# Differential attention: its outputs turned by head group and four tiles, and the output stage run as one sequence of 16 tiles

## The chip, the cores and the metric

The kernel runs on one core of a Trainium2 chip. The metric is the time of one execution on the device in microseconds (us), lower is better. The core has a matmul engine (TensorE, PE in the rows, with its weight loads as PEld), VectorE (DVE), ScalarE (ACT), GpSimd (POOL) and SyncE (SP), which issues the DMAs.

## The reference

The input is 16 sequences of 1024 tokens with 256 features. Four blocks follow one another, each on a layernorm of its input and added to it: a local attention, a feed-forward block, a differential attention, the same feed-forward block. The change lies in the third, which is this (cut):

```python
def _L0_attn_b_ref(x, Wq, Wk, Wv, Wo, lambda_q1, ..., subln_g):
    H, hd = 16, 8
    q = rope((x @ Wq).reshape(b, s, 2 * H, hd))      # 32 heads of 8
    k = rope((x @ Wk).reshape(b, s, 2 * H, hd))
    v = (x @ Wv).reshape(b, s, H, 2 * hd)            # 16 heads of 16
    probs = softmax(q k^T / sqrt(hd))                # per head, 1024 x 1024
    w = probs[:, :, 0] - lam * probs[:, :, 1]        # heads in pairs
    attn = w @ v
    rms = rsqrt(mean(attn * attn, -1) + EPS)
    attn = attn * rms * subln_g * (1.0 - LAMBDA_INIT)
    return attn.reshape(b, s, 256) @ Wo
```

## The kernel before, in words

A loop runs eight times, each time over a pair of sequences (`PB` = 2). A sequence has 8 tiles of 128 tokens (`T`), a pair 16 (`TT`). In each round stand layernorm, local attention, layernorm, `ffn`, layernorm, `diff_project` and `diff_attention`, `diff_output`, layernorm, `ffn`. The order of work on each engine is written out by hand; engines wait for each other by semaphores.

**The rotation.** `diff_attention` works on 16 groups (`PB * NG`) of four heads (`G`), eight per sequence. A clock of steps `e` runs over all of them, 32 steps (`STEPS`) to a group, 512 in all (`LAST`). In a step TensorE makes, alternating, two matmuls of exponent scores (`exp_scores`, L1203) for this step and two of max scores (`max_scores`, L1181) for the step `AHEAD` = 39 later, and then half of the value matmuls of a unit (`values`, eight per step in the rows, L1221). ScalarE makes two exponentials per step (L1339), VectorE one maximum over 1024 scores (L1257). In 39 steps at the end there are no max scores any more. The unnormalised outputs with their row sums stand in one PSUM bank per half group; ScalarE copies them to `oT` (`keep_output`, L1359), features in partitions, two steps into the next group. The next value matmuls wait for that copy. Once in a group, GpSimd cuts the maxima in three parts (`cut`), TensorE turns them (L1189) and SyncE stores them.

**Turning the outputs.** 32 units are needed in a pair to bring outputs back to tokens in partitions: each is four transposes of 128 x 128 into one PSUM bank (`turned_heads`, L1004). Before, a unit is one tile of 128 tokens for four head groups, so it needs all eight of a sequence's groups in two halves, numbered `j` = 0 to 15. Behind the transposes comes a chain: divide by the row sums, subtract lambda times the second head of each pair, mean square, inverse root, multiply, write to `attended`.

- The 16 units of the first sequence are *early*: they stand in the rotation at steps 6 and 15 of groups 4 to 11 (`EARLY`). The turn takes one of the three banks of the exponent scores, ScalarE copies it out (`keep_raw`, L1348), and GpSimd does the whole chain (`early`, L1305 to L1316).
- 8 units of the second sequence stand in the tail, from step `ALONE` on, one in four steps (`output_step`). Their chain is shared: VectorE `combine` (L1016, L1018, L1025), GpSimd `square` (L1032), VectorE `mean_square` (L1036, L1038), GpSimd `inverse_root` (L1042), VectorE `normalise` (L1050).
- The last 8 stand in `diff_output`, with the same chain.

**The output stage.** `diff_output` is a block of its own: for each tile TensorE transposes the two 128-column halves of `attended` (`features`, L1385), ScalarE copies them to `aT` (`keep`, L1450), TensorE multiplies by `wo` in two accumulating matmuls (`project`, L1393, four instructions in the rows), VectorE adds to `x` (`residual`, L1415) and takes the layernorm statistics (`statistics`, L1420). Its loop runs over tiles `t` of both sequences at once, the second two tiles behind. Each sequence has one PSUM bank for its projection, so `project(b, t)` waits for `residual(b, t - 1)`:

```python
for t in range(T + 5):
    if t < T:
        combine(v, T + t)
    if 1 <= t <= T:
        mean_square(v, T + t - 1)
    if 2 <= t < T + 2:
        normalise(v, T + t - 2)
    if 2 <= t < T + 2:
        residual(0, t - 2)
    if 3 <= t < T + 3:
        statistics(0, t - 3)
    if 4 <= t < T + 4:
        residual(1, t - 4)
```

## Time and profile before

| | |
|---|---|
| Median of three runs | 9148.5 us (9129.78 to 9150.74) |
| Profiled execution | 9143.53 us, its span 9141.9 us |
| TensorE, matmuls | 7776.9 us busy, 85% |
| VectorE | 7227.1 us, 79% |
| ScalarE | 6201.5 us, 68% |
| GpSimd | 2700.3 us, 30% |
| TensorE's mean granted clock | 0.924 |

Times in a timeline are microseconds from the start of the span. A row of several instructions (x4) gives the start of the first and the time to the end of the last; matmuls are pipelined, so the next row can start before it ends. In brackets stands how long the engine was idle before the row, and what released it. A granted clock of 1.0 is 2.4 GHz, 0.5 is 1.2 GHz.

### The profile page before, as it was taken

The numbers are of one execution on the slowest core, as the hardware profiler recorded it, in microseconds if no ns is written. First come the engines' busy times: TensorE is split into PE (matmuls) and PEld (weight loads), VectorE is DVE, ScalarE is ACT, GpSimd is POOL, SyncE is SP. The second block draws the span as 40 slices with busy tenths as digits, with TensorE's granted clock in tenths as the row PEclk, the third lists the DMA queues.
The fourth block names the chain that finished last, engine by engine and source line by source line (L and its number), as shares of the span: only waits on it lengthen the run. The fifth ranks groups of instructions, "written<-read, shape, count | busy, mean of one in ns | idle before, by whom it ended". The sixth has DMA issues, their size and how long they took to land. (4 is left out here: it accounts for less than half of the span.)

```text
span 9141.9 us, 163324 instructions
## 1 busy us (share of the span) xinstructions
PE 7776.9 (85%) x65408; PEld 2851.3 (31%) x65408; DVE 7227.1 (79%) x9490; ACT 6201.5 (68%) x11410; POOL 2700.3 (30%) x3046
## 2 busy tenths in 40 slices
PE   6799877998779987799877998779977799777997
PEld 3222342223422234222342223422234222342223
DVE  5899558995589955899558995589955899558995
ACT  4499544995449954499544995449955499554995
POOL 3233241332413324133241332413324133241322
PEclk9899987999879998799988999889999799897998
DMA  0100001000010000100001000010000100001000
GB/s 28 42 23 23 10 10 42 23 23 10 10 42 23 23 12 9 42 23 23 14 7 45 23 20 16 5 46 23 19 17 4 46 23 19 19 1 46 23 19 19
DMA packets 216827, 204.98 MB, mean 22 GB/s; under 512 B 105783, under 2 KB 141111, under 8 KB 216055
## 3 DMA queue, kind: packets, MB, share of 16 engines
q1 hardware_dynamic: 216060, 194.46, 7.4%
q8 instruction: 519, 8.50, 0.4%
q14 instruction: 248, 2.02, 0.1%
HBM read 123.83 MB, written 67.37 MB: 21 GB/s over the span
## 5 line engine op out<-in xcount | busy, mean ns | idle before, releaser
L1257 DVE TENSOR_REDUCE mfull<-ps 128x1 f32<-128x1024 f32 x4096 | 4692.9, 1217 | 225.1 <-PE ps L1181 220.7
L1339 ACT ACTIVATE work<-ps 128x512 f32<-128x512 f32 x8192 | 4385.6, 597 | 346.9 <-PE ps L1203 225.0
L1221 PE MATMUL ps<-work,vbuf 128*32 128x256 f32 x32768 | 2623.2, 392 | 116.6 <-ACT hh L1359 116.6
L1181 PE MATMUL ps<-kop,qop 48*128 48x512 bf16 x8192 | 2507.2, 394 | 59.1 <-DVE mfull L1257 51.7
L1203 PE MATMUL ps<-qop,kop 51*128 51x512 bf16 x8192 | 2489.2, 384 | 0.0
L1221 PEld LDWEIGHTS ps<-work,vbuf 128*32 128x32 f32 x32768 | 654.3, 108 | 1800.9 <-issue 896.0
L1203 PEld LDWEIGHTS ps<-qop,kop 51*128 51x128 bf16 x8192 | 482.2, 93 | 1649.6 <-ACT work L1339 1585.9
L1287 POOL CAST mpart<-mfull 128x32 bf16<-128x32 f32 x128 | 27.0, 211 | 2541.6 <-DVE mfull L1257 2363.6
L1305 POOL TENSOR_TENSOR work<-work,none 128x16 f32<-128x16 f32 x128 | 371.7, 2904 | 1014.4 <-ACT work L1348 1014.4
L263 PE MATMUL ps<-ident,hh 128*128 128x128 f32 x1024 | 200.0, 373 | 510.4 <-DVE hh L233 510.4
L416 POOL TENSOR_TENSOR hh<-work,hmask 128x1024 f32<-128x1024 f32 x256 | 522.1, 2065 | 129.7 <-PE ps L344 129.6
L1181 PEld LDWEIGHTS ps<-kop,qop 48*128 48x128 bf16 x8192 | 473.2, 94 | 218.3 <-DVE mfull L1257 190.5
L816 POOL TENSOR_TENSOR work<-work,vbuf 128x1024 f32<-128x1024 f32 x64 | 194.6, 3041 | 884.0 <-DVE work L731 884.0
L272 ACT COPY hh<-ps 128x512 f32<-128x512 f32 x128 | 75.1, 587 | 492.1 <-PE ps L263 492.1
L518 ACT COPY vbuf<-qop 32x512 f32<-32x512 f32 x512 | 315.5, 616 | 116.7 <-DVE qop L461 107.2
L609 PE MATMUL ps<-work,w 128*128 128x512 f32 x768 | 371.3, 623 | 12.9 <-ACT work L674 6.6
L1016 DVE RECIPROCAL work<-ps 128x16 f32<-128x16 f32 x128 | 32.8, 257 | 411.6 <-PE ps L1004 411.6
L263 PEld LDWEIGHTS ps<-ident,hh 128*128 128x128 f32 x1024 | 174.1, 196 | 534.3 <-DVE hh L233 520.7
L882 PE MATMUL ps<-wv,hh 128*128 128x256 f32 x512 | 215.0, 561 | 141.1 <-DVE work L911 141.1
L361 PE MATMUL ps<-vbuf,work 128*32 128x128 f32 x4096 | 162.0, 306 | 182.2 <-ACT hh L523 175.3
L729 DVE TENSOR_TENSOR hh<-work,vbuf 128x1024 f32<-128x1024 f32 x128 | 156.2, 1220 | 172.4 <-ACT vbuf L667 172.4
L1393 PE MATMUL ps<-wo,work 128*128 128x256 f32 x512 | 191.0, 515 | 113.4 <-DVE x L1415 113.4
(163 smaller groups left out, 9125.6 us busy)
## 6 DMA issues: line engine op xcount, KB each, us to landing
qop<-scratch SPq DMA_DIRECT2D x512, 64.0 KB
scratch<-work SPq DMA_DIRECT2D x32, 768.0 KB, 3.6
scratch<-hh SPq DMA_DIRECT2D x32, 768.0 KB, 4.6
kop<-scratch SPq DMA_DIRECT2D x256, 96.0 KB
vbuf<-in_x SPq DMA_DIRECT2D x9, 2048.0 KB, 8.3
qop<-scratch SPq DMA_DIRECT2D x512, 32.0 KB
kop<-scratch SPq DMA_DIRECT2D x256, 64.0 KB
out<-x SPq DMA_DIRECT2D x64, 256.0 KB, 2.1
```

The costliest lines, as they stand in the source:

```text
L263: mm = pe.transpose(ps[:, 4 * (t // T) + c * NB + t % T // 4, at:at + P], h[:, t, c * P:(c + 1) * P], ident[:, :])
L416: pool.tensor_tensor(kx[i % len(kx)], qkT[:, b, 2 + c, tb * P:(tb + 1) * P][:, None, :].to_broadcast([P, LC, P]), hmask[:, :, None].to_bro ...
L518: act.copy(PT[t % 2][r, :, r], pr[t % 2][r]).then_inc(s_pa, 1)
L609: mm = pe.matmul(ps[:, 2 * n, :], w2[:, c, :], a1[n][:, c, :], start=c == 0, stop=c == C - 1)
L816: pool.tensor_tensor(U[n], U[n], cr[0][n][:, None, :].to_broadcast([P, C, HALF]), ALU.mult).then_inc(s_q, 1)
L882: mm = pe.matmul(ps[:, 4 + t // 2, (t % 2) * D:(t % 2 + 1) * D], hT[:, b, c, t * P:(t + 1) * P], wv[:, c, :], start=c == 0, stop=c == C - 1)
L1181: pe.matmul(ps[:, b + n, :], qop[r:r + KQ, s, i, t * P:(t + 1) * P], kop[r:r + KQ, s, i, half(n)], start=True, stop=True).then_inc(s_ms, 1)
L1203: pe.matmul(ps[:, bank, :], kop[r:r + KM, s, i, t * P:(t + 1) * P], qop[r:r + KM, s, i, half(n)], start=True, stop=True).then_inc(s_sc, 1)
L1221: mm = pe.matmul(ps[VW * i:VW * (i + 1), OB, cols], vp[:, b, t, (G * gl + i) // 2, :], prob[:, u % PS, i, cols], start=t == 0 and part == ...
L1257: v.tensor_reduce(mfull[:, g % 2, r // ROWS, i * T + t:i * T + t + 1], ps[:, b:b + NB, :].rearrange("p b n -> p (b n)"), AX.X, ALU.max).th ...
L1305: link(pool.tensor_tensor(erz, y[:, :, LD], none[:, :], ALU.pow))
L1339: act.activation(prob[:, u % PS, hl, :], ps[:, EB[slot % len(EB)], :], ACT.Exp, scale=scale).then_inc(s_ex, 1)
```

## The change

A unit is now one head group for four tiles (`side` 0 or 1 of its sequence), so it can be turned as soon as its own group is finished. Early are all units of groups 0 to 13 (`FIRST` = 14): 28 of them, each pair at steps 6 and 15 of the group that follows. The units of group 14 stand at steps 6 and 10 of the last group (`LATE`), those of group 15 in `diff_output`. There the loop runs over 16 tiles in one sequence, features two tiles ahead of projections, with two banks for the projections and four for the features; all but two units' chains are gone from it.

```diff
+        FIRST = PB * NG - 2
         def output_bank(j):
...
-        def turned_heads(pe, bank, j):
-            g0, t = NG // 2 * (j // T), j % T
-            for g in range(g0, g0 + NG // 2):
-                mm = pe.transpose(ps[:, bank, (g - g0) * P:(g - g0 + 1) * P],
-                                  oT[:, g, t * P:(t + 1) * P], ident[:, :])
+        def turned_heads(pe, bank, g, side):
+            for t in range(T // 2):
+                at = (side * T // 2 + t) * P
+                mm = pe.transpose(ps[:, bank, t * P:(t + 1) * P], oT[:, g % NG, at:at + P], ident[:, :])
             return mm
...
         def turn_output(pe, j):
-            if j % T >= 2:
+            if j >= 2:
                 pe.wait_ge(s_nm, j - 1)
-            turned_heads(pe, output_bank(j), j).then_inc(s_tp, 1)
+            turned_heads(pe, output_bank(j), FIRST + j // 2, j % 2).then_inc(s_tp, 1)
...
-        def heads_of(b, t, c):
-            return attended[:, b, t, c * P:(c + 1) * P].rearrange("p (v d) -> p v d", d=LD)
+        def normalised(eng, g, side, by, root):
+            b, cols = g // NG, slice(g % NG * 2 * LD, (g % NG + 1) * 2 * LD)
+            dst = attended[:, b, side * T // 2:(side + 1) * T // 2, cols].rearrange("p t (v d) -> p t v d", d=LD)
+            factor = root.rearrange("p (t v) -> p t v", v=2)[:, :, :, None].to_broadcast([P, T // 2, 2, LD])
+            return eng.tensor_tensor(dst, by.rearrange("p (t v) d -> p t v d", v=2), factor, ALU.mult)
         def normalise(v, j):
-            t, c = j % T, j // T
             v.wait_ge(s_pw, j + 1)
-            v.tensor_tensor(heads_of(1, t, c), diff[j % 3],
-                            rr[:, j, :][:, :, None].to_broadcast([P, HV, LD]), ALU.mult).then_inc(s_an, 1)
+            normalised(v, FIRST + j // 2, j % 2, diff[j % 3], rr[:, j, :]).then_inc(s_an, 1)
...
             HQ = HALF // 2
-            ALONE = LAST - AHEAD + 4
-            EARLY = [STEPS * g + o for g in range(NG // 2, NG // 2 + NG) for o in (6, 15)]
+            EARLY = [STEPS * (g + 1) + o for g in range(FIRST) for o in (6, 15)]
+            LATE = [STEPS * (FIRST + 1) + o for o in (6, 10)]
             scale = DD ** -0.5
...
-            def output_step(e):
-                j = e - ALONE
-                return j // 4 if j % 4 == 0 and 0 <= j < 4 * T else None
             def value_tile(e):
...
                     def early_turn(j):
-                        pe.wait_ge(s_oe, NB * NG // 2 * (j // T + 1))
-                        turned_heads(pe, bank_for(turn_slot(j)), j).then_inc(s_sc, 1)
+                        pe.wait_ge(s_oe, NB * (j // 2 + 1))
+                        turned_heads(pe, bank_for(turn_slot(j)), j // 2, j % 2).then_inc(s_sc, 1)
...
                                 values(tile_due(e, part), part)
-                        if output_step(e) is not None:
-                            if output_step(e) == 0:
+                        if e in LATE:
+                            if e == LATE[0]:
                                 pe.wait_ge(s_mts, GROUPS)
-                            turn_output(pe, output_step(e))
+                                pe.wait_ge(s_oe, NB * (FIRST + 1))
+                            turn_output(pe, LATE.index(e))
...
                         reduce(m)
-                    for j in range(T + 2):
-                        if j < T:
-                            combine(v, j)
-                        if 1 <= j <= T:
-                            mean_square(v, j - 1)
-                        if j >= 2:
-                            normalise(v, j - 2)
+                    for step in (combine, mean_square, normalise):
+                        for j in range(2):
+                            step(v, j)
...
                         link(pool.tensor_tensor(err, esv, nhalf[:, 0:HV], ALU.pow))
-                        link(pool.tensor_tensor(heads_of(0, j % T, j // T), ediff,
-                                                err[:, :, None].to_broadcast([P, HV, LD]), ALU.mult))
+                        link(normalised(pool, j // 2, j % 2, ediff, err))
...
                             early(EARLY.index(e))
-                    for j in range(T + 1):
-                        if j < T:
-                            square(pool, j)
-                        if j >= 1:
-                            inverse_root(pool, j - 1)
+                    for step in (square, inverse_root):
+                        for j in range(2):
+                            step(pool, j)
...
-            s_wt, s_we, s_wm, s_wx = ([sem(f"do_{n}{b}") for b in range(PB)] for n in ("wt", "we", "wm", "wx"))
+            s_wt, s_we, s_wm, s_wx = (sem(f"do_{n}") for n in ("wt", "we", "wm", "wx"))
             with nc.Block() as block:
...
                 def _(pe):
-                    def features(b, t, c):
-                        if b:
-                            pe.wait_ge(s_an, c * T + t + 1)
-                        if t >= 2 and c == 0:
-                            pe.wait_ge(s_we[b], t - 1)
-                        pe.transpose(ps[:, 4 + 2 * b + t % 2, c * P:(c + 1) * P], attended[:, b, t, c * P:(c + 1) * P],
-                                     ident[:, :]).then_inc(s_wt[b], 1)
+                    def features(t):
+                        if t == T:
+                            pe.wait_ge(s_an, 4)
+                        if t >= 4:
+                            pe.wait_ge(s_we, t - 3)
+                        for c in range(C):
+                            mm = pe.transpose(ps[:, 4 + t % 4, c * P:(c + 1) * P],
+                                              attended[:, t // T, t % T, c * P:(c + 1) * P], ident[:, :])
+                        mm.then_inc(s_wt, 1)
-                    def project(b, t):
-                        pe.wait_ge(s_we[b], t + 1)
-                        if t >= 1:
-                            pe.wait_ge(s_wx[b], t)
+                    def project(t):
+                        pe.wait_ge(s_we, t + 1)
+                        if t >= 2:
+                            pe.wait_ge(s_wx, t - 1)
                         for c in range(C):
-                            mm = pe.matmul(ps[:, 2 + b, 0:D], aT[:, b, c, t * P:(t + 1) * P],
+                            mm = pe.matmul(ps[:, 2 + t % 2, 0:D], aT[:, t // T, c, t % T * P:(t % T + 1) * P],
                                            wo[:, c, :], start=c == 0, stop=c == C - 1)
-                        mm.then_inc(s_wm[b], 1)
+                        mm.then_inc(s_wm, 1)
-                    for t in range(T + 3):
-                        if t < T:
-                            turn_output(pe, T + t)
-                            for c in range(C):
-                                features(0, t, c)
-                        if 1 <= t <= T:
-                            project(0, t - 1)
-                        if 2 <= t < T + 2:
-                            for c in range(C):
-                                features(1, t - 2, c)
-                        if t >= 3:
-                            project(1, t - 3)
+                    for j in (2, 3):
+                        turn_output(pe, j)
+                    for t in range(TT + 2):
+                        if t < TT:
+                            features(t)
+                        if t >= 2:
+                            project(t - 2)
...
                 def _(v):
-                    def residual(b, t):
-                        tt = T * b + t
-                        v.wait_ge(s_wm[b], t + 1)
-                        v.tensor_tensor(x[:, tt, :], x[:, tt, :], ps[:, 2 + b, 0:D], ALU.add).then_inc(s_wx[b], 1)
-                    def statistics(b, t):
-                        tt = T * b + t
-                        v.wait_ge(s_wx[b], t + 1)
-                        v.bn_stats(st[:, tt, :], x[:, tt, :])
-                    for t in range(T + 5):
-                        if t < T:
-                            combine(v, T + t)
-                        if 1 <= t <= T:
-                            mean_square(v, T + t - 1)
-                        if 2 <= t < T + 2:
-                            normalise(v, T + t - 2)
-                        if 2 <= t < T + 2:
-                            residual(0, t - 2)
-                        if 3 <= t < T + 3:
-                            statistics(0, t - 3)
-                        if 4 <= t < T + 4:
-                            residual(1, t - 4)
-                        if t >= 5:
-                            statistics(1, t - 5)
+                    def residual(t):
+                        v.wait_ge(s_wm, t + 1)
+                        v.tensor_tensor(x[:, t, :], x[:, t, :], ps[:, 2 + t % 2, 0:D], ALU.add).then_inc(s_wx, 1)
+                    def statistics(t):
+                        v.wait_ge(s_wx, t + 1)
+                        v.bn_stats(st[:, t, :], x[:, t, :])
+                    for step in (combine, mean_square):
+                        for j in (2, 3):
+                            step(v, j)
+                    for t in range(TT + 1):
+                        if t < TT:
+                            residual(t)
+                        if t >= 1:
+                            statistics(t - 1)
+                        if t in (1, 2):
+                            normalise(v, t + 1)
...
                 def _(pool):
-                    for t in range(T + 1):
-                        if t < T:
-                            square(pool, T + t)
-                        if t >= 1:
-                            inverse_root(pool, T + t - 1)
+                    for step in (square, inverse_root):
+                        for j in (2, 3):
+                            step(pool, j)
...
                 def _(act):
-                    def keep(b, t):
-                        act.wait_ge(s_wt[b], C * (t + 1))
-                        act.copy(aT[:, b, :, t * P:(t + 1) * P],
-                                 ps[:, 4 + 2 * b + t % 2, 0:D].rearrange("p (c n) -> p c n", c=C)).then_inc(s_we[b], 1)
-                    for t in range(T + 2):
-                        if t < T:
-                            keep(0, t)
-                        if t >= 2:
-                            keep(1, t - 2)
+                    for t in range(TT):
+                        act.wait_ge(s_wt, t + 1)
+                        act.copy(aT[:, t // T, :, t % T * P:(t % T + 1) * P],
+                                 ps[:, 4 + t % 4, 0:D].rearrange("p (c n) -> p c n", c=C)).then_inc(s_we, 1)
```

TensorE in the rotation, at steps 5 and 6 of group 1 (L1004 and L1006 are the turn; L1203, L1181, L1221 before are L1200, L1178, L1218 now). Before:

```order
L1203 MATMUL ps<-qop,kop 128x512
L1181 MATMUL ps<-kop,qop 128x512
L1221 MATMUL ps<-work,vbuf 32x256 x4
L1203 MATMUL ps<-qop,kop 128x512
L1181 MATMUL ps<-kop,qop 128x512
```

and now:

```order
L1200 MATMUL ps<-qop,kop 128x512
L1178 MATMUL ps<-kop,qop 128x512
L1218 MATMUL ps<-work,vbuf 32x256 x4
L1006 MATMUL ps<-ident,hh 128x128 x4
L1200 MATMUL ps<-qop,kop 128x512
L1178 MATMUL ps<-kop,qop 128x512
```

A turn has moved in between the value matmuls of a step and the scores of the next, here and at step 15, in groups 1 to 3 and 12 to 14 too.

TensorE at the start of `diff_output` (L1004, now L1006, turns outputs; L1385, now L1376, are features; L1393, now L1385, projections). Before:

```order
L1004 MATMUL ps<-ident,hh 128x128 x4
L1385 MATMUL ps<-ident,work 128x128 x2
L1004 MATMUL ps<-ident,hh 128x128 x4
L1385 MATMUL ps<-ident,work 128x128 x2
L1393 MATMUL ps<-wo,work 128x256 x2
L1004 MATMUL ps<-ident,hh 128x128 x4
L1385 MATMUL ps<-ident,work 128x128 x2
L1393 MATMUL ps<-wo,work 128x256 x2
```

and now:

```order
L1006 MATMUL ps<-ident,hh 128x128 x8
L1376 MATMUL ps<-ident,work 128x128 x6
L1385 MATMUL ps<-wo,work 128x256 x2
L1376 MATMUL ps<-ident,work 128x128 x2
L1385 MATMUL ps<-wo,work 128x256 x2
```

Six of eight turns have left the block; the other two stand ahead of everything.

VectorE in `diff_output`, from the chain of one new unit to the next (L1016, L1018, L1025 are `combine`, L1036 and L1038 `mean_square`, L1050 `normalise`, L1415 `residual`, L1420 `statistics`). Before:

```order
L1016 RECIPROCAL work<-ps 128x16
L1018 TENSOR_TENSOR work<-ps,work 128x256
L1025 SCALAR_TENSOR_TENSOR work<-work,nlam 128x128
L1036 TENSOR_REDUCE work<-work 128x8
L1038 TENSOR_SCALAR work<-work 128x8
L1050 TENSOR_TENSOR work<-work 128x128
L1415 TENSOR_TENSOR x<-x,ps 128x256
L1420 BN_STATS st<-x 128x6
L1415 TENSOR_TENSOR x<-x,ps 128x256
L1420 BN_STATS st<-x 128x6
```

and now, from the second `mean_square` on (L1037, L1039; L1049 is `normalise`, L1401 `residual`, L1405 `statistics`):

```order
L1037 TENSOR_REDUCE work<-work 128x8
L1039 TENSOR_SCALAR work<-work 128x8
L1401 TENSOR_TENSOR x<-x,ps 128x256 x2
L1405 BN_STATS st<-x 128x6
L1049 TENSOR_TENSOR work<-work 128x4x32
L1401 TENSOR_TENSOR x<-x,ps 128x256
L1405 BN_STATS st<-x 128x6
L1049 TENSOR_TENSOR work<-work 128x4x32
L1401 TENSOR_TENSOR x<-x,ps 128x256
L1405 BN_STATS st<-x 128x6
```

After that only residuals and statistics alternate, where six more rounds of the chain stood between them.

## Rows read from the trace of the kernel before

**Rows 1.** View by stretch: rotation, output stage of the second pair.

```profile
1530.00:2142.70 612.70, 590.81 (x6176) 155.40 (x6173) 555.67 (x522) 566.83 (x1087) 165.53 (x283) 0.99 0.07 19
2142.70:2190.40 47.70, 32.08 (x128) 24.97 (x128) 24.59 (x80) 5.97 (x16) 16.27 (x16) 0.79 0.00 1
```

**Rows 2.** Timeline of TensorE in the rotation (start us, length us, engine, line, operation).

```profile
1685.32 0.64 PE L1221 MATMUL ps<-work,vbuf 128*32 128x256 f32 x8 [0.48 <-ACT hh L1359]
...
1687.54 0.64 PE L1221 MATMUL ps<-work,vbuf 128*32 128x256 f32 x8
1688.11 0.66 PE L1004 MATMUL ps<-ident,hh 128*128 128x128 f32 x4
...
1689.23 0.64 PE L1221 MATMUL ps<-work,vbuf 128*32 128x256 f32 x8
```

**Rows 3.** Timeline of the rotation's tail: TensorE, and ScalarE's last output copy.

```profile
2132.68 0.64 PE L1221 MATMUL ps<-work,vbuf 128*32 128x256 f32 x8
...
2134.37 0.64 PE L1221 MATMUL ps<-work,vbuf 128*32 128x256 f32 x8
...
2142.05 0.59 ACT L1359 COPY hh<-ps 128x512 f32<-128x512 f32 x1 [1.19 <-PE ps L1221]
```

**Rows 4.** Timeline of TensorE in the output stage.

```profile
2142.95 0.63 PE L1004 MATMUL ps<-ident,hh 128*128 128x128 f32 x4 [0.96 <-PEq L1133]
2143.41 0.38 PE L1385 MATMUL ps<-ident,work 128*128 128x128 f32 x2
...
2144.28 1.10 PE L1393 MATMUL ps<-wo,work 128*128 128x256 f32 x4
...
2173.34 1.56 PE L1393 MATMUL ps<-wo,work 128*128 128x256 f32 x4 [2.10 <-DVE x L1415]
2174.69 0.63 PE L1385 MATMUL ps<-ident,work 128*128 128x128 f32 x2
2175.12 1.92 PE L1393 MATMUL ps<-wo,work 128*128 128x256 f32 x4
2176.83 0.82 PE L1004 MATMUL ps<-ident,hh 128*128 128x128 f32 x4
...
2184.53 0.38 PE L1385 MATMUL ps<-ident,work 128*128 128x128 f32 x2
2184.75 1.03 PE L1393 MATMUL ps<-wo,work 128*128 128x256 f32 x4
2185.62 0.38 PE L1385 MATMUL ps<-ident,work 128*128 128x128 f32 x2
...
2188.09 1.10 PE L1393 MATMUL ps<-wo,work 128*128 128x256 f32 x4 [0.61 <-DVE x L1415]
```

**Rows 5.** Timeline of VectorE in the output stage.

```profile
2148.38 0.41 DVE L1415 TENSOR_TENSOR x<-x,ps 128x256 f32<-128x256 f32 x1
...
2171.07 0.26 DVE L1016 RECIPROCAL work<-ps 128x16 f32<-128x16 f32 x1 [3.49 <-PE ps L1004]
...
2172.79 0.41 DVE L1415 TENSOR_TENSOR x<-x,ps 128x256 f32<-128x256 f32 x1
...
2187.53 0.42 DVE L1415 TENSOR_TENSOR x<-x,ps 128x256 f32<-128x256 f32 x1 [0.62 <-PE ps L1393]
...
2189.23 0.42 DVE L1415 TENSOR_TENSOR x<-x,ps 128x256 f32<-128x256 f32 x1 [0.95 <-PE ps L1393]
2189.57 0.74 DVE L1420 BATCH_NORM_STATS2 st<-x 128x6 f32<-128x256 f32 x2
```

**Rows 6.** Timeline of GpSimd in the rotation: a unit's chain, the next chain.

```profile
1689.33 2.92 POOL L1305 TENSOR_TENSOR work<-work,none 128x16 f32<-128x16 f32 x1 [14.44 <-ACT work L1348]
...
1698.11 0.40 POOL L1316 TENSOR_TENSOR work<-work 128x128 f32<-128x128 f32 x1
1699.87 2.91 POOL L1305 TENSOR_TENSOR work<-work,none 128x16 f32<-128x16 f32 x1 [1.36 <-ACT work L1348]
```

**Rows 7.** Groups by line: busy us, mean ns of one, idle us before and releaser.

```profile
L1348 ACT COPY work<-ps 128x272 f32<-128x272 f32 x128 | 49.4, 386 | 39.4 <-PE ps L1004 39.4
```

## The prediction

> **What bounds the kernel now.** I read the page's head first (no engine is busy for more than 85% of the span, so the change must be priced stage by stage), then busy time by stretch, then the timeline of the second of the eight pairs, engine by engine. The view by stretch gives the length, the busy time of TensorE, its weight loads, VectorE, ScalarE and GpSimd, and TensorE's granted clock. The two stretches that it touches are the rotation (1530.0 to 2142.7 us) and the output stage (2142.7 to 2190.4 us). In the rotation TensorE is busy 590.8 of 612.7 us, and its clock is granted at 0.99; in the output stage it is busy 32.1 of 47.7 us at 0.79, so it sits idle for a third of the time and runs at 1.2 GHz for part of it [rows 1].
>
> In the rotation one step lasts 1.11 us (two of them from the value matmuls at 1685.32 to those at 1687.54). The step that holds a turn of attention outputs lasts 1.69 us (1687.54 to 1689.23): its four transposes push everything behind them back by 0.58 us [rows 2]. So the matmul queue sets the pace there, and nothing hides a turn. In the tail, where the max scores have ended, a step with a turn lasts 1.69 us as well (2132.68 to 2134.37) [rows 3].
>
> The output stage is the slow one. One round of its loop makes one turn and takes a tile of each sequence through features and projection, and in each TensorE waits for `residual` on VectorE before the second sequence's projection: 2.10 us at 2173.34, for one [rows 4]. VectorE is late because `residual` of the first sequence stands in its queue behind the whole chain of a new unit (`combine`, `mean_square`, `normalise`): L1016 starts at 2171.07 and the residual L1415 at 2172.79, 1.72 us later [rows 5]. The matmuls of a round themselves are short at 2.4 GHz: features to projection 0.22 us (2184.53 to 2184.75), projection to next features 0.87 us (2184.75 to 2185.62), so 1.09 us a tile. At 1.2 GHz they take 0.43 and 1.71 us, 2.14 us a tile (2174.69, 2175.12, 2176.83) [rows 4].
>
> **The change, part by part.**
>
> *Turns in the rotation.* Both versions turn 32 units of four transposes in a pair. Before, 16 are early, 8 are in the tail and 8 in the output stage; now 28 are early, 2 in the tail and 2 in the output stage. The rotation holds 30 instead of 24, so it grows by 6 x 0.58 = 3.5 us. Bounds: 6 x 0.46 = 2.8 us by the turn in the output stage (2142.95 to 2143.41 [rows 4]) and, if each of the 12 added early turns also cost ScalarE's copy of 0.39 us, 3.5 + 4.7 = 8.2 us. I take 3.5, because the early turn of [rows 2] already carries that copy [rows 7] and costs the same as one in the tail, which has none. The order within the turn (four tiles of one head group, not four groups of one tile) leaves count and shape alone.
>
> *Waits of the added turns.* Each now follows the output copy of its own group, where before four groups lay between. The last value matmul that waited for that copy goes at 1685.32, and the first turn of the group stands at 1688.11, 2.8 us later [rows 2]. The wait is over by then: nothing. GpSimd's chain for a unit runs 1689.33 to 1698.51, 9.2 us, and the next one begins 1.36 us after it [rows 6]. The added chains keep those places, steps 6 and 15 of 32, with `cut` of the maxima at step 24 behind them, so what holds in groups 4 to 11 holds in the new ones. `normalised` writes four pieces of 32 columns instead of one of 128; were its 0.40 us to double, the 1.36 us would still cover it. In the six groups that get chains anew, GpSimd was idle.
>
> *Tail.* Two units at step 6 and 10 of the last group, so VectorE and GpSimd finish their chains well before ScalarE's last copy ends at 2142.64 (2142.05 + 0.59 [rows 3]). Nothing.
>
> *Output stage.* Before, it lasts from 2142.64 to the end of the last statistics, 2189.57 + 0.74 = 2190.31: 47.7 us [rows 5]. Now:
> - TensorE starts at 2142.95 as before. Two turns at 0.46 (2142.95 to 2143.41 [rows 4]): 0.92. The first projection starts 0.87 after the first features (2143.41 to 2144.28, with ScalarE's copy between): projection 0 at 2144.74, projection 1 at 2144.74 + 1.09 = 2145.83.
> - Projection 2 needs residual 0. Before, the first residual starts at 2148.38, behind three units' `combine`; now two stand ahead of it, which takes the 1.72 us of one unit out of the queue: 2146.7. TensorE goes on 0.56 us after a residual starts (2187.53 to 2188.09 [rows 4, 5]): 2147.3, where its own queue would have come to it at 2146.9, a wait of 0.4 us.
> - From there nothing holds TensorE. Per tile VectorE needs at most 0.41 us for the residual and 0.37 for the statistics (0.74 for two) [rows 5], and ScalarE's one copy fits into the 0.87 us from features to projection above, against 1.09. A projection's bank comes back in time: the residual starts about 0.26 us after the last matmul has issued (2188.09 + 0.87 = 2188.96; 2189.23) and TensorE goes 0.56 later, 0.82 in all, while the next tile covers 0.22 + 0.87 + 0.22 = 1.31 us.
> - `normalise` of the last two units ends at the latest two units after that first residual, 2146.7 + 2 x 1.72 = 2150.1. The first features of the second sequence go after projection 5, near 2151.4. This wait costs nothing.
> - Projections 3 to 13: 11 x 1.09 = 12.0; the last two without features 2 x 0.87 = 1.7: projection 15 at 2161.0. From there to the end of statistics 2.22 us (2188.09 to 2190.31): 2163.3.
> That is 20.6 us; 0.4 for handovers that I cannot see makes 21.0. Bounds: 20.2 without the early wait and the allowance; 40.5 at 1.2 GHz throughout (below).
>
> *Clock.* The sum takes 2.4 GHz. In the output stage of before, with waits of 2.10 us in TensorE's queue [rows 4], its mean is 0.79, and matmuls of the same kind issue in 0.43 us after such a wait and in 0.22 late in the stage; in the rotation, where TensorE is busy for 96% of the time, it is 0.99 [rows 1]. The new stage has one gap of about 1 us at the start, as before, one of 0.4, and then none. A rule of the Trainium skill speaks against this: "TensorE: Matmul & The Clock Gate", section "A second HAM failure mode: psum-queue depth-cycling", says that cycling through PSUM banks in each iteration can leave gaps small and many enough for the clock to swing between its two levels. The new stage does cycle two and four banks. By that rule the sum would come out as rival 1; the rotation cycles seven banks and keeps its clock, which is why I hold to the row.
>
> *What stays.* Layernorm, ffn, local attention, the projections and all DMAs are untouched; SP's queue holds the same.
>
> **Sum.** Per pair 47.7 - 21.0 - 3.5 = 23.2 us; x 8 = 186 us. I take off 2 us because not every pair need be as long as this one: 184 us. The profiled execution took 9143.5 us, so 8960 us. The median of the three runs lies 5 us higher; I say **8962 us**, 2.0% less.
>
> **Rivals.**
> 1. *The clock falls in the output stage.* At the share of low clock of before (mean 0.79) the stage's 19 us of matmul work become 19 / 0.79 = 24: +5 us a pair, +40: about 9002 us. At 1.2 GHz throughout, a tile costs 2.14 instead of 1.09, over some 18 tile lengths +19 us a pair, +152: 9114 us, still 0.4% faster. For: the clock of before does swing there. Against: it fell after waits that are gone. Chance 0.15, nearly all of it on the mild form.
> 2. *The turns cost more in the rotation.* If every early turn waited for its output copy by the 0.48 us of [rows 2], 28 x 0.48 = 13 us a pair, +108: 9070 us. Against: 2.8 us of distance. Chance 0.03.
> 3. *Slower: the hand-back stays in series.* If a projection in the new stage still waits 2.10 us for its residual, as in every period of before, now with every tile, a tile costs 1.09 + 2.10 = 3.2 us; 16 x 3.2 + 4 = 55 us, 7.5 more than now, and with the 3.5 of the rotation 11 us a pair: +88, about 9232 us. It decides from a tile length of (47.7 - 3.5 - 4) / 16 = 2.5 us on. For: projections use two banks and wait for the residual two tiles back. Against: that wait came from the chains queued ahead of the residual, of which two are left, both at the start. Chance 0.02.
> 4. *The change does nothing there*, because something that I don't see bounds the stage, 9140 us: 0.02.
>
> **How the numbers follow.** Forecast 0.78, rivals 0.15, 0.03, 0.02, 0.02. The low end is the sum with the lower bounds, 0.8 us a pair for the stage and 0.8 for the turns (-13), and the spread of the runs shown (14 us below the profiled one): 8938. The high end takes in the mild clock case and some more of low clock, 9035. A measurement here can tell about 0.3% from no change, 27 us. Faster by more than that: forecast, rivals 1 and 2, 0.96; within it 0.02; slower 0.02.
>
> **What would show it.** Right: in the profile of the changed kernel the stage from ScalarE's last output copy to the last statistics takes about 21 us, with projections (L1385) 1.09 us apart, a granted clock near 1.0 in it and no wait of 2.10 us; groups 1 to 3 and 12 to 14 of the rotation are 1.16 us longer each, and the tail has two steps of 1.69 us. Wrong: a tile length of 2.1 us (clock), a wait for `residual` at each tile (rival 3), or a wait before the turns in the rotation.

## The result, and the profile after

| | before | after |
|---|---|---|
| median | 9149.62 us (4 runs, 9129.78 to 9152.19) | 8992.63 us (4 runs, 8968.44 to 9000.3) |
| profiled execution | 9143.53 us | 8998.98 us, its span 8997.5 us |

The ratio is 0.983, with a 95% interval of 0.9812 to 0.9849: 157 us less, where 186 us were forecast. The time, 8992.6 us, lies inside the range of 8938 to 9035 us and 31 us above the 8962 us forecast. The changed kernel is 1.7% faster, and a ratio of 1 lies far outside the interval. What has to be found out is where these 31 us went (29 by the differences). The two profiled executions are 144.5 us apart and not 157, so they show some 13 us more missing than the medians do.

The busy time by stretch of the changed kernel, for the same pair as [rows 1], columns as there (length, busy time and count of TensorE, weight loads, VectorE, ScalarE and GpSimd, TensorE's granted clock, DMA share, GB/s). First the output stage, then the rotation with what leads up to its first exponential:

```profile
2140.60:2161.00 20.40, 18.91 (x104) 15.80 (x104) 15.30 (x44) 5.77 (x16) 4.04 (x4) 1.00 0.00 0
1524.00:2140.60 616.60, 594.37 (x6202) 157.51 (x6200) 547.04 (x487) 570.97 (x1099) 252.57 (x415) 0.99 0.07 19
```

The stage went from 47.70 to 20.40 us, and its clock from 0.79 to 1.00, which is 2.4 GHz throughout. TensorE is busy there for 93% of the time, against 67% before. GpSimd's sixteen steps have become four.

The timeline of all engines from the last output copy (L1350) into the stage answers to [rows 4, 5]. Columns: start, length, engine, line and operation, tiles, count, and the idle time before with its releaser:

```profile
2139.94 0.59 ACT L1350 COPY hh<-ps 128x512 f32<-128x512 f32 x1 [1.19 <-PE ps L1218]
2140.84 1.06 PE L1006 MATMUL ps<-ident,hh 128*128 128x128 f32 x8 [0.96 <-PEq L1130]
...
2142.58 1.13 PE L1385 MATMUL ps<-wo,work 128*128 128x256 f32 x4
...
2143.77 1.03 PE L1385 MATMUL ps<-wo,work 128*128 128x256 f32 x4
...
2144.53 0.74 DVE L1401 TENSOR_TENSOR x<-x,ps 128x256 f32<-128x256 f32 x2
...
2145.09 1.10 PE L1385 MATMUL ps<-wo,work 128*128 128x256 f32 x4
...
2146.25 1.03 PE L1385 MATMUL ps<-wo,work 128*128 128x256 f32 x4
...
2150.57 0.42 DVE L1401 TENSOR_TENSOR x<-x,ps 128x256 f32<-128x256 f32 x1 [0.33 <-PE ps L1385]
2150.59 1.03 PE L1385 MATMUL ps<-wo,work 128*128 128x256 f32 x4
...
2151.67 1.03 PE L1385 MATMUL ps<-wo,work 128*128 128x256 f32 x4
```

Two things are to be seen. The projections (L1385) stand 1.08 to 1.09 us apart once the stage runs (2150.59, 2151.67), and now VectorE waits for TensorE (0.33 us), not TensorE for VectorE: the 2.10 us of [rows 4] are gone. The projection of tile 2 at 2145.09 comes 1.32 us behind that of tile 1 at 2143.77, so the one wait at the start that the sum allowed for is about 0.2 us instead of 0.4.

In the rotation the added turns look like the old ones. The timeline of TensorE around the first turn of group 1, where none stood before, and of GpSimd behind it, answers to [rows 2, 6]:

```profile
1568.10 0.64 PE L1218 MATMUL ps<-work,vbuf 128*32 128x256 f32 x8 [0.48 <-ACT hh L1350]
...
1570.32 0.64 PE L1218 MATMUL ps<-work,vbuf 128*32 128x256 f32 x8
1570.88 0.66 PE L1006 MATMUL ps<-ident,hh 128*128 128x128 f32 x4
1571.47 0.39 PE L1200 MATMUL ps<-qop,kop 51*128 51x512 bf16 x1
...
1572.01 0.64 PE L1218 MATMUL ps<-work,vbuf 128*32 128x256 f32 x8
```

```profile
1572.11 2.91 POOL L1299 TENSOR_TENSOR work<-work,none 128x16 f32<-128x16 f32 x1 [14.44 <-ACT work L1339]
...
1580.90 0.40 POOL L1049 TENSOR_TENSOR work<-work 128x128 f32<-128x128 f32 x1
1582.66 2.91 POOL L1299 TENSOR_TENSOR work<-work,none 128x16 f32<-128x16 f32 x1 [1.35 <-ACT work L1339]
```

The step with a turn lasts 1.69 us (1570.32 to 1572.01). The last value matmul that waited for the group's output copy (the 0.48 us) goes 2.8 us before the turn, and the turn has no wait of its own. GpSimd's chain still takes 9.2 us, its last write 0.40 us although it now goes in four pieces, and 1.36 us are left to the next. By the starts of ScalarE's exponentials, groups 1 to 3, 12 and 13 of this pair are 1.1 to 1.3 us longer than before, group 14 is 0.58 longer (one of the tail's turns stood in it before) and the last group is 2.9 us shorter (39.9 to 36.9 us from its first exponential to its last), which is five turns of 0.58 less.

**The stages of the whole loop.** From the first and last rows of each stage (statistics L244, first exponential, last output copy, last statistics of the output stage) follow these lengths, means over the eight pairs in us; the last column, up to L244 of the next round, over seven:

| | layernorm, local | layernorm, ffn | layernorm, project | rotation | output stage | layernorm, ffn, back to the top |
|---|---|---|---|---|---|---|
| before | 133.2 | 112.0 | 117.0 | 612.5 | 47.4 | 116.5 |
| after | 135.4 | 112.4 | 117.5 | 615.9 | 20.4 | 119.5 |
| difference | +2.2 | +0.4 | +0.5 | +3.3 | -27.0 | +2.9 |

The two stages that were priced give 27.0 - 3.3 = 23.7 us a pair, against 23.2 forecast. The rest was taken as unchanged and is not: 8 x (2.2 + 0.4 + 0.5) + 7 x 2.9 = 45 us. 8 x 23.7 - 45 = 145 us is the difference of the two spans (9141.9 and 8997.5 us, 144.4).

**The last column.** The idle time of VectorE before the round's first instruction (L242), all executions of it, by what ended it (us, times). Before:

```profile
  PEq L1472: 34.7, 7
```

After:

```profile
  issue: 55.4, 7
```

"issue" means that nothing in the profile held the engine. One execution of it in the timeline of VectorE, before and after:

```profile
2305.59 1.17 DVE L242 BATCH_NORM_AGGREGATE mv<-st 128x2 f32<-128x6 f32 x16 [4.97 <-PEq L1472]
```

```profile
2279.18 1.17 DVE L242 BATCH_NORM_AGGREGATE mv<-st 128x2 f32<-128x6 f32 x16 [7.89 <-issue]
```

That is 3 us a round, 20.7 us over the seven. The records of control instructions say where: from the branch that closes the loop to the first instruction of the next round (a hint to prefetch, which stands at the top of each round on every engine) VectorE takes 0.52 to 0.59 us before and 2.82 to 3.50 us after, while the other engines take 0.25 to 0.47 us in both. VectorE's loop body has shrunk from 1257 to 1173 instructions, because the chains of twelve units are no longer VectorE's but GpSimd's.

**The first three columns.** They differ with TensorE's granted clock, and within one execution too. By stretch, changed kernel: one pair's projection at a low and one at a higher clock, then two local attentions:

```profile
4774.27:4891.28 117.01, 85.45 (x242) 37.81 (x243) 93.03 (x90) 25.20 (x30) 35.31 (x18) 0.73 0.23 75
5891.22:6003.21 111.99, 80.23 (x242) 35.01 (x243) 92.93 (x90) 25.21 (x30) 35.31 (x18) 0.82 0.23 78
...
4526.23:4661.59 135.36, 104.09 (x1184) 69.58 (x1184) 82.39 (x189) 66.51 (x108) 78.57 (x37) 0.85 0.00 1
5646.73:5779.76 133.03, 100.88 (x1184) 66.45 (x1184) 81.86 (x189) 66.50 (x108) 78.61 (x37) 0.90 0.01 1
```

The kernel before, two local attentions:

```profile
3446.80:3579.47 132.67, 100.44 (x1184) 66.17 (x1184) 81.88 (x189) 66.57 (x108) 78.59 (x37) 0.90 0.01 1
5723.31:5858.89 135.58, 103.82 (x1184) 69.49 (x1184) 82.48 (x190) 66.57 (x108) 78.56 (x37) 0.85 0.01 1
```

The same instructions take 132.7 or 135.6 us in both kernels, with TensorE's busy time 3 us apart and everybody else's nearly equal. Before, seven of eight pairs were of the short kind; after, one of eight.

### The profile page after: what moved, and what is told of

The parts are those of the page before. It is cut to its first block and busy times, and to the rows that moved or that the text cites. A ratio compares the mean times of both kernels' runs of the same rounds, so it can differ in the third digit from the quotient of the medians.

```text
span 8997.5 us, 163868 instructions
## 1 busy us (share of the span) xinstructions
PE 7715.0 (86%) x65408; PEld 2815.5 (31%) x65408; DVE 7091.0 (79%) x8914; ACT 6231.5 (69%) x11506; POOL 3298.5 (37%) x4006
## 5 line engine op out<-in xcount | busy, mean ns | idle before, releaser
L1218 PE MATMUL ps<-work,vbuf 128*32 128x256 f32 x32768 | 2623.2, 392 | 118.6 <-ACT hh L1350 118.6
L1178 PE MATMUL ps<-kop,qop 48*128 48x512 bf16 x8192 | 2506.0, 395 | 58.6 <-DVE mfull L1255 51.7
L1200 PE MATMUL ps<-qop,kop 51*128 51x512 bf16 x8192 | 2487.8, 384 | 0.0
L1299 POOL TENSOR_TENSOR work<-work,none 128x16 f32<-128x16 f32 x224 | 650.4, 2904 | 1775.4 <-ACT work L1339 1775.4
L1218 PEld LDWEIGHTS ps<-work,vbuf 128*32 128x32 f32 x32768 | 654.3, 108 | 1807.0 <-issue 916.7
L1200 PEld LDWEIGHTS ps<-qop,kop 51*128 51x128 bf16 x8192 | 478.4, 93 | 1634.4 <-ACT work L1330 1577.2
L1178 PEld LDWEIGHTS ps<-kop,qop 48*128 48x128 bf16 x8192 | 470.9, 94 | 217.8 <-DVE mfull L1255 190.8
L1309 POOL TENSOR_TENSOR work<-work,nhalf 128x8 f32<-128x8 f32 x224 | 373.8, 1669 | 18.7
L255 POOL TENSOR_TENSOR rstd<-rstd,nhalf 128x16 f32<-128x16 f32 x32 | 93.0, 2908 | 513.7 <-DVE rstd L244 513.7
```

The costliest lines, as they stand in the source:

```text
L1178: pe.matmul(ps[:, b + n, :], qop[r:r + KQ, s, i, t * P:(t + 1) * P], kop[r:r + KQ, s, i, half(n)], start=True, stop=True).then_inc(s_ms, 1)
L1200: pe.matmul(ps[:, bank, :], kop[r:r + KM, s, i, t * P:(t + 1) * P], qop[r:r + KM, s, i, half(n)], start=True, stop=True).then_inc(s_sc, 1)
L1218: mm = pe.matmul(ps[VW * i:VW * (i + 1), OB, cols], vp[:, b, t, (G * gl + i) // 2, :], prob[:, u % PS, i, cols], start=t == 0 and part == ...
L1299: link(pool.tensor_tensor(erz, y[:, :, LD], none[:, :], ALU.pow))
L1309: link(pool.tensor_tensor(err, esv, nhalf[:, 0:HV], ALU.pow))
```

## The experiments

The kernel before ran beside the others each time, so its median moves a little: 9156.73 us (7 runs) for e1 to e4, 9145.4 (9 runs) for e5 to e7, 9163.36 (one run) for e8 and e9. The theory that was tested first: VectorE's 3 us are a fetch of instructions at the back edge (the branch from the end of the loop to its top), caused by where the shorter body ends, not by the work in it.

**e1: the head of the loop put at slot 0.** A slot is a position in the engine's instruction stream, counted modulo 256 (a fetch block, below). Nothing else changes.

```diff
-        with nc.Fori(0, PAIRS, hint_back_edge=True) as q:
+        with nc.Fori(0, PAIRS, hint_back_edge=True, head_slot={mybir.EngineType.DVE: 0}) as q:
```

> The changed kernel, with VectorE's loop body loaded from another place (slot 0 of a fetch block); no instruction is added or taken. Theory A: the 3.0 us that VectorE needs in the changed kernel from the loop's closing branch to the first instruction of the next round (0.5 us in the kernel before) is a fetch of instructions that comes too late because of where the closing branch stands in a fetch block. Then it falls to about 0.5 us, the stretch from the last statistics of the output stage to the next round's layernorm from 119.4 to 116.5 us, and the time by about 20 us, to 8970 us. Rival B: it comes from the change's own instructions in the loop, wherever they stand; then it stays at 3.0 us and the time at 8990 us.

Measured: 8969.26 us (4 runs, 8964.76 to 8973.06), ratio to the kernel before 0.9794 (0.9778 to 0.981). From branch to next instruction 0.52 to 0.59 us in every round, and the last column is back at 116.4 us. VectorE's idle time before L242:

```profile
  PEq L1444: 34.5, 7
  issue: 3.6, 1
```

The single "issue" of 3.6 us is the entry into the loop, paid once. Medians: 23 us less than the changed kernel. The 3 us a round hang on the position of the code alone.

**e2: the length of the body brought back.** 84 instructions (168 waits on a value long reached, two to an instruction) ahead of VectorE's late chains, where it waits anyway.

```diff
                     for m in range(LAST):
                         reduce(m)
+                    for k in range(168):
+                        v.wait_ge(s_mr, LAST - k)
                     for step in (combine, mean_square, normalise):
```

> The changed kernel with 84 instructions more on VectorE (waits that have long been met), placed in the tail of the rotation where VectorE is idle, so that its loop has as many instructions as before (1257). Theory A: the branch stands where it stood before, and VectorE goes on after 0.5 us instead of 3.0; stretch of 116.5 us. Rival B: 3.0 us stay. Rotation and output stage as in the changed kernel (616 and 20.4 us).

Measured: 8955.91 us (one run), body 1257 instructions as before, 0.5 to 0.6 us at every back edge, last column 116.4 us. More instructions, less time.

**e3: the kernel before, with 172 instructions added.** The body is then 1429 long, which is 1173 + 256, so its end falls on the same slot of a block as that of the changed kernel.

```diff
                         if j >= 2:
                             normalise(v, j - 2)
+                        if j < T:
+                            for k in range(44 if j < 4 else 42):
+                                v.wait_ge(s_mr, LAST - k)
```

> The kernel before with 172 such waits more on VectorE, in its idle gaps in the tail, so that its closing branch stands at the same place of a fetch block as in the changed kernel (1429 instructions = 1173 + 256). Theory A: the stall of 3.0 us appears in the kernel before too, and its stretch from the last statistics to the next layernorm grows from 116.5 to 119.4 us. Rival B: 0.5 us as in the kernel before. Output stage 47.7 us in both.

Measured: 9162.42 us (one run). VectorE's idle time before L242:

```profile
  issue: 54.8, 7
```

The stall of the changed kernel (55.4 us in seven rounds), in the kernel that never had it; the last column is 119.4 us. The output stage took 46.3 us (47.4 before) and the whole time lies within what the kernel before showed beside it (9135.26 to 9164.75 us), so the stall is read from its own gap and not from the time. With e1 and e2 it is shown from both sides. A second reading: local attention took 134.6 us on average here against 133.2, though its code is the old one. So a good part of the +2.2 us in the first column comes without the change's work.

**e4: one bank for the projections instead of two.** Each projection then waits for the residual of the tile before.

```diff
-                        if t >= 2:
-                            pe.wait_ge(s_wx, t - 1)
+                        if t >= 1:
+                            pe.wait_ge(s_wx, t)
...
-                            mm = pe.matmul(ps[:, 2 + t % 2, 0:D], ...
+                            mm = pe.matmul(ps[:, 2, 0:D], ...
```

> The changed kernel with one PSUM bank instead of two for the projections of the output stage, so that each projection waits for the residual of the tile just before. Theory: the tile length is set by TensorE's own 1.08 us only while the hand-back (0.26 + 0.56 us after the matmuls) is hidden behind the next tile; with one bank a tile becomes 0.87 + 0.26 + 0.56 = 1.7 us, the stage 20.4 + 13 x 0.62 = 28 to 30 us, if the clock stays high; if the gap of 0.6 us a tile lets the clock fall, tiles of 2.5 us and a stage of up to 42 us. Rival: the second bank does not matter, since features stand between two projections: 20.4 us.

Measured: 9066.55 us (one run). The stage takes 30.7 us, a little over the 28 to 30 expected, a tile 1.70 to 1.71. The timeline of TensorE, and the stage by stretch:

```profile
2153.17 1.10 PE L1385 MATMUL ps<-wo,work 128*128 128x256 f32 x4 [1.16 <-DVE x L1401]
2154.11 0.38 PE L1376 MATMUL ps<-ident,work 128*128 128x128 f32 x2
2154.87 1.10 PE L1385 MATMUL ps<-wo,work 128*128 128x256 f32 x4 [0.39 <-DVE x L1401]
```

```profile
2148.60:2179.30 30.70, 22.21 (x104) 16.02 (x104) 15.30 (x44) 5.78 (x17) 4.04 (x4) 1.00 0.00 0
```

Each tile is 1.70 - 1.09 = 0.61 us longer (the idle time in brackets is 0.39 of it), worth 10.2 us a pair with the longer wait at the start: the second bank is what takes the hand-back out of series. And the clock stays at 1.00 although TensorE is busy for only 72% of the stage, hardly more than the 67% at 0.79 before. Busy share alone does not tell the two apart; what does, these rows leave open.

**e5: one transpose of four in each early turn.** Leaves out three of four tiles in every early unit; ScalarE's copy keeps its size.

```diff
-        def turned_heads(pe, bank, g, side):
-            for t in range(T // 2):
+        def turned_heads(pe, bank, g, side, tiles=T // 2):
+            for t in range(tiles):
...
-                        turned_heads(pe, bank_for(turn_slot(j)), j // 2, j % 2).then_inc(s_sc, 1)
+                        turned_heads(pe, bank_for(turn_slot(j)), j // 2, j % 2, 1).then_inc(s_sc, 1)
...
-                        act.copy(raw[j % 2], src[:, :, 0:LD + 1]).then_inc(s_ex, 1)
+                        act.copy(raw[j % 2].rearrange("p (t k) w -> p t k w", k=4),
+                                 src[:, None, :, :].to_broadcast([P, 4, 4, LD + 1])).then_inc(s_ex, 1)
```

> The changed kernel with one transpose instead of four in each of the 28 early turns; ScalarE copies the one turned tile four times into the same buffer (same size of copy), GpSimd's chain is unchanged. What is left out: three of four tiles of these outputs. Theory: the price of a turn in the rotation is TensorE's transposes, so that three of four gone take 28 x 0.44 = 12.3 us from the rotation (616.0 to about 604 us a pair). Rival: ScalarE's copy of 0.39 us, hidden behind them, takes their place; then a turn still costs 0.3 us and the rotation falls by 7 to 8 us only, to 608. A second rival, that GpSimd's chains or their contention set the price: 616 stay.

Measured: 8910.61 us (one run). The rotation takes 607.1 us, 8.8 less, 0.31 us for each of 28 turns. By the starts of ScalarE's exponentials a group of 32 steps takes 37.23 us without turns (kernel before), 38.39 with two, and 37.78 here: 0.58 and 0.28 us a turn. The time falls between the two theories, nearer to the rival's 608. TensorE's timeline around the same turn as above:

```profile
1555.07 0.64 PE L1218 MATMUL ps<-work,vbuf 128*32 128x256 f32 x8
1555.64 0.33 PE L1006 MATMUL ps<-ident,hh 128*128 128x128 f32 x1
1555.90 0.39 PE L1200 MATMUL ps<-qop,kop 51*128 51x512 bf16 x1
...
1556.43 0.64 PE L1218 MATMUL ps<-work,vbuf 128*32 128x256 f32 x8
```

From the first transpose to the next scores TensorE takes 0.26 us with one transpose (1555.64 to 1555.90) and 0.59 with four (1570.88 to 1571.47), and neither row of scores shows a wait. So a turn does not cost four equal parts: three transposes less save 0.33 us, 28 x 0.33 = 9.2 us against 8.8 measured, and the 0.26 that is left stands in TensorE's own queue. The theory's number missed because it took 0.44 of the 0.58 off; the rival's number came close, but no wait for ScalarE's copy is needed to explain it. ScalarE has no idle time before its copy of this turn (0.29 us in the changed kernel), so a limit set by ScalarE may lie close below; that was not tried.

**e6: eight units in the output stage again, with the new order of tiles.** Eight of the 32 units stand in the output stage, as before, one per tile (the other 24 are early, none is in the tail), with their chains on VectorE and GpSimd; the sequence of 16 tiles and the banks stay.

```diff
-        FIRST = PB * NG - 2
+        FIRST = PB * NG - 4
...
-                    for j in (2, 3):
-                        turn_output(pe, j)
                     for t in range(TT + 2):
+                        if t < T:
+                            turn_output(pe, t)
                         if t < TT:
                             features(t)
...
-                    for t in range(TT + 1):
-                        if t < TT:
-                            residual(t)
-                        if t >= 1:
-                            statistics(t - 1)
-                        if t in (1, 2):
-                            normalise(v, t + 1)
+                    for t in range(TT + 3):
+                        if t < T:
+                            combine(v, t)
+                        if 1 <= t <= T:
+                            mean_square(v, t - 1)
+                        if 2 <= t <= T:
+                            normalise(v, t - 2)
+                        if t == T:
+                            normalise(v, T - 1)
+                        if 2 <= t < TT + 2:
+                            residual(t - 2)
+                        if t >= 3:
+                            statistics(t - 3)
```

> The changed kernel with 8 units in the output stage, as in the kernel before (24 early, none in the tail), each turned ahead of the features of one of the first 8 tiles, its chain queued ahead of the residuals; the order of 16 tiles, two banks for projections and four for features stay. It splits the gain of the output stage between the chains that left and the new order. Theory that the chains ahead of the residuals set the stage: the first 8 tiles cost 2.4 us each by VectorE's queue (1.7 for the chain, 0.7 for residual and statistics), the stage 8 x 2.4 + 8 x 1.1 + 3 = 31 us and more if the clock falls in the waits (37). Rival, that the old order with one bank a sequence was the loss: 20.4 + 6 x 0.5 of turns = 24 us. Rotation 612.5 us, as before.

Measured: 9063.14 us (one run), the stage 34.7 us on average, between the 31 and the 37 us expected, the rotation 612.4. TensorE's timeline, and the stage by stretch:

```profile
2144.01 1.10 PE L1377 MATMUL ps<-wo,work 128*128 128x256 f32 x4 [0.64 <-DVE x L1393]
...
2158.60 0.69 PE L1368 MATMUL ps<-ident,work 128*128 128x128 f32 x2 [6.67 <-DVE work L1049]
2159.08 1.91 PE L1377 MATMUL ps<-wo,work 128*128 128x256 f32 x4
2160.78 0.64 PE L1368 MATMUL ps<-ident,work 128*128 128x128 f32 x2
2161.21 1.37 PE L1377 MATMUL ps<-wo,work 128*128 128x256 f32 x4
```

```profile
2137.10:2171.30 34.20, 23.94 (x128) 19.47 (x128) 24.15 (x79) 6.55 (x17) 16.20 (x16) 0.90 0.00 1
```

Projections 2 to 5 wait 0.33 to 0.64 us each for a residual queued behind a chain, and then the features of the second sequence wait 6.67 us for the last `normalise`. So the new order and its banks take the stage from 47.4 to 34.7 us, and the chains' leaving it from 34.7 to 20.4, taken in this order and with the clock that each was granted (0.79, 0.90, 1.00). Behind the 6.67 us gap the same matmuls take 1.91 and 1.37 us instead of 1.03: the clock had fallen. No stall at the back edge (34.6 us in seven rounds, as before), with a body of 1201 instructions.

**e7: the kernel of e2 again, timed in five rounds.**

> The changed kernel with 84 met waits more on VectorE (as e2), now timed in rounds: its closing branch goes on after 0.5 us. By the stretches of its trace a pair is 1115 us against 1121 in the changed kernel: 8 x 2.9 = 23 us for the branch, the rest by the clock of the other stages, which differs from run to run: 8960 to 8975 us, 0.2 to 0.4% below the changed kernel.

Measured: 8964.87 us (5 runs, 8952.98 to 8966.1), ratio to the kernel before 0.9801 (0.9787 to 0.9814). Its slowest run lies below the changed kernel's fastest (8968.44), and the medians are 28 us apart. It beats both kernels.

**e8, e9: two more positions.** e1's edit with 106 and with 110 in place of 0. The closing branch stands 1172 instructions behind the head, 4 x 256 + 148; so it stands at slot 148 in e1, at 254 in e8, at 2 in e9. The four instructions between 106 and 110 tell apart whether it is the branch's own slot that matters (at the start of a block) or the body's length.

> As e1, with VectorE's loop starting at slot 106 of a fetch block of 256 instructions, so that the closing branch, 1172 instructions on, stands at slot (106 + 1172) mod 256 = 254, at the very end of a block. Theory C: the stall needs a closing branch in the first slots of a block, because the block with the branch and the branch's target are then wanted one right after the other; at slot 254 it goes on after 0.5 us. Theory D: a branch near either side of the boundary stalls; 3 us here too.

> As e1, with VectorE's loop starting at slot 110, so that the closing branch stands at slot (110 + 1172) mod 256 = 2, just behind the start of a block. Theory C and theory D: the stall of about 3 us is there in every round. If it goes on after 0.5 us, neither holds and what makes the place of e3, e4 and the changed kernel a bad one stays open.

Measured: e8 8977.64 us, e9 8986.26 (one run each). VectorE's idle time before L242, e8 and then e9:

```profile
  PEq L1444: 34.4, 7
  issue: 3.8, 1
```

```profile
  issue: 52.1, 7
```

e8 takes 0.50 to 0.54 us at each back edge, e9 2.3 to 3.4. Same body, four slots apart (the head moves by the same four, in the middle of its block). The two times differ by 8.6 us only, less than seven such stalls: the stages ahead of the rotation were 1.0 us a pair shorter in e9, and e8 pays 3 us on entering the loop; so here too the gap itself is read and not the time. The stall comes with the closing branch at slot 2 of a block and not at 148 or 254; how many slots behind the start are bad was not tried. Every other kernel fits: the changed one, e3, e4 and e5 stall and their bodies have the same remainder by 256; before, e2 and e7 (84 slots later) and e6 (28 slots later) don't. Which slot the changed kernel's loop begins at by itself, the records don't say.

A rule of the Trainium skill fits this. "Runtime: NRT & Kernel Launch", section "Instruction fetch mechanics", says that most engines hold two blocks of 256 instructions, and that a taken branch to a target outside them waits for a fetch. The traces agree in so far as their DMA records of kind "instruction" tell the two groups apart: within 8 us of VectorE's closing branch, queue 14 moves five packets in every round of the five kernels that stall (the changed one, e3, e4, e5, e9), and three or four in every round of the six that don't. The stall is about 2.5 us beyond the 0.5 of an undisturbed back edge. For which engine a packet is, and what becomes of the stall without the prefetch hint, which all of these kernels have, no run here shows.

## Why the prediction was right, and where it was not

**Right in direction, mechanism and the two stages it priced.**
- *Turns in the rotation:* +3.5 us a pair forecast, +3.3 measured. The step with a turn is 1.69 us, as forecast; e5 shows that the transposes set it. The upper bound of 8.2, each added early turn paying ScalarE's copy besides, did not come about.
- *Waits of the added turns, GpSimd's chain:* nothing forecast, none seen: 2.8 us of distance and 1.36 us of slack, both as before.
- *Tail:* nothing beyond its turns forecast; the last group is 2.9 us shorter, five turns of 0.58. Of the groups that were to grow by 1.16 us, group 14 grew by 0.58 only, since one tail turn had stood in it; the sum of 30 turns against 24 already had that right.
- *Output stage:* 21.0 us forecast, 20.44 measured, the same in all eight pairs. The tile length of 1.09 us was exact. The allowance of 0.4 us for unseen handovers was not needed, and the early wait was about 0.2 instead of 0.4. Of the two terms behind the reduction, by e6 order and banks carried 12.7 us and the chains' leaving 14.3.
- *Clock of the stage:* 2.4 GHz taken, 1.00 granted. Rival 1 fell. The swing of the clock that the prediction cited from the Trainium skill ("TensorE: Matmul & The Clock Gate", "A second HAM failure mode: psum-queue depth-cycling") was not seen here: not with two and four banks in the changed kernel, and not in e4, where each tile had 0.39 us of idle time.
- *Rival 3*, the hand-back in series, is what e4 builds. With one bank it costs 0.61 us a tile and not the rival's 2.10, since the residual is no longer behind a chain; even then the kernel is faster than before (9066.55 us).

**Wrong: "What stays".** The prediction took layernorm, ffn, local attention and projections as untouched, and so at no cost: 0 us in the sum, where 45 us were measured between the profiled executions. The step that failed is the one from "no instruction of these stages changes" to "their time does not change". The 45 us have two parts.
- *The back edge of the loop*, 2.9 us in each of seven rounds, 20 us, of which the branch itself shows 2.3 to 2.9. No instruction of these stages changed, but VectorE's body became 84 instructions shorter, so its closing branch moved to another slot of a fetch block. e1, e2, e3, e8 and e9 show in both directions that the place of the code makes the stall; that the changed kernel's own slot is just behind the start of a block follows from e8 and e9 and is not on record. The sum had counted instructions only by their duration, never by where the code ends.
- *The clock elsewhere*, +3.1 us a pair, 25 us in these two executions. The same instructions of local attention take 133 or 135.5 us by the clock granted there (0.90 or 0.85), and the projection 111.6 to 120.6 over all runs. In the profiles of the nine experiments the three stages together are 0.6 to 2.5 us a pair longer than before (1.5 in e1, 1.4 in e7), so part of the 3.1 belongs to this one execution. e3 moved local attention to 134.6 us with the old code and only waits added. So this is not work that the change added, but what decides which pair runs at the low level stays open: the changed kernel and those that differ from it only in padding or in the position of code (e1, e2, e7, e8, e9) came out between 134.4 and 135.4 us. What is shown is that no kernel tried here had as many short pairs as the kernel before, which had seven of eight.

Without the first part the forecast holds: e1, with all of the change's work and no stall, took 8969.3 us, and e7 8964.9, beside 8962 forecast; as ratios to the kernel before, 0.9794 and 0.9801 beside 0.980. Two things in the number were luck or slips. The sum as written, 9143.5 - 184 and 5 more for the median, gives 8964.5 us and not 8962. And the result lies in the range because its high end had been set for a low clock in the output stage, which did not come; nothing in the range had been meant for the stages called untouched.

## What to carry to other kernels

Price an edit in a loop also by what it does to the length of each engine's body: when a stage that nobody touched grows by a fixed 2 to 3 us a round, look at the idle time before the round's first instruction, and at whether it says "issue". Then try another slot for the head of the loop, so that the closing branch does not stand right behind the start of a block, or pad, and do it before small gains are judged, since it was worth 23 to 28 us here. And where a hand-back between two engines sets the pace, look first at what is queued ahead of the answer: moving chains away was worth 14 us a pair, and the second bank for the projection 10 (the two are taken from different kernels and do not add up), while the moved turns cost only what their matmuls take.

## What was not expected of the hardware

- This loop's back edge costs VectorE 0.50 to 0.59 us with its closing branch at slot 254 or 148 of a block, and 2.3 to 3.4 us at slot 2, with the prefetch hint in place in all of them. Adding 84 instructions that do nothing made the kernel 28 us faster (medians 8992.6 and 8964.9).
- TensorE kept a granted clock of 1.00 through a stage of 30.7 us in which it was busy 72% of the time and idle for about 0.39 us before nearly every projection; after one gap of 6.67 us it ran slower for some 4 us (matmul rows of 1.91 and 1.37 us, then 1.03).
- A turn's price is not proportional to its transposes: TensorE goes on 0.26 us after the start of one, and 0.59 us after the start of four (e5 and the changed kernel).
- One and the same stretch of code, in one execution, takes 112.0 or 117.0 us by the clock that is granted there (0.82 or 0.73). Differences of one or two microseconds in a stage that was not edited are no evidence about the edit.
